# A decoder layer whose query projection is done in seven block products instead of eight

## The chip, the cores and the metric

The kernel runs on one core of one Trainium2 chip. The metric is the device time of one execution in microseconds (us), lower is better. A few words of the text: TensorE, VectorE, ScalarE, GpSimd and SyncE are the core's engines (PE, DVE, ACT, POOL and SP in the rows; PEld is the load of weights into TensorE). Each has a queue of its own that it works off in order, and they wait for one another by semaphores. SyncE issues all the transfers here. PSUM is TensorE's output memory, in 8 banks of 128 x 512 float32; SBUF is the working memory.

## The reference

One pre-norm decoder layer over 2 batches of 512 tokens, 1024 wide: self-attention, a quantised product with a context, and a mixture of 64 low-rank experts. What matters for the change is the attention:

```python
q = (hidden_states @ Wq.T).reshape(b, s, H, D)          # 32 heads of 128
kc, vc = hidden_states @ Wk_down.T, hidden_states @ Wv_down.T
k, v = k_cmp @ Wk_up.T, v_cmp @ Wv_up.T                 # from the latents: 8 heads of 128
scores = q @ k.T / sqrt(D)                              # causal, 4 query heads share a key head
out = softmax(scores) @ v
x = x + out @ Wo.T
```

After it come `x + fake_quant(layernorm(x)) @ fake_quant(ctx)` and `x + ffn(layernorm(x))`, which the change leaves as they are.

## The kernel before

**Numbers.** Every float32 operand of the attention is held as two float16 parts, a rounded one ("hi", made by ScalarE, L594) and the remainder ("lo", made by VectorE from the source and the hi part, L855). `split_product` (L1245) multiplies hi by hi, hi by lo and lo by hi, so each block of 128 rows takes three matmuls.

**Stages.** First the layer norm, the turning of its result into `h_t` and the down projection to the latents `lat` (TensorE until 69 us in the profile). Then eight groups, one a key head, the first and the last written out and the six in the middle in a loop; then the rest of the output projection, and the two later layers.

**A group** has 8 steps (`UNITS`), one for each of its four query heads and two batches. In step u TensorE does in this order (`group`, L1394):

- `scores(g, u)`: 12 matmuls into banks 0 to 2, which need the queries of unit u and the keys;
- `outputs(g, u - 2)`: probabilities times values for the unit of two steps ago, 15 matmuls into bank 5;
- two chunks of the output projection, `wo_chunk`: 6 matmuls of 512 columns each, over a pair of heads that is complete, mostly of the group before;
- `q_product(u + 2)`: the queries that are used two steps later, 24 matmuls of 512 columns;
- two more chunks.

Chunks, query products and the keys and values share four banks in rotation (`GEN_BANK`); a product waits until the one four uses back is read. In step 1 the group's values come in ahead of the chunks (two products `v_product`), in step 7 the keys of the next group (`k_product`). The order of the uses is written down by `step_uses`. In the first group there are no chunks before step 6, and in the last one no query products after step 5.

**Beside it.** VectorE in step u: `maxima(u)` (scores and mask to `prob`, row maxima, then `neg_max`, L1012), `p_split(u - 1)` (the remainder of the probabilities, 1280 columns), the add of the first chunk to `x_sb` (`wo_add`, L993), `inverses(u)` (L980), `o_split(u - 2)`, the add of the second chunk, a weight split of 1024 columns in most steps (`wq_sb` in even, `wo_sb` in odd ones), at times a context rounding or a smaller split, the query remainder, and two adds. ScalarE does the hi parts and the exponentials in between. GpSimd multiplies the exponentials by the inverses (L565), clips a context chunk (L546) in two steps and adds one to a column sum (L554) in two. The probabilities are then turned by two DMA transpositions a unit (`turn`, hi and lo), both on SyncE's queue, which also loads weights and context chunks between them.

**At the group's ends.** `scores(g, u + 1)` waits for `neg_max` of u (its banks), `outputs` for both transpositions and for `o_split` of the unit before (bank 5), and `outputs` of the first unit for the values.

## Time and profile before

| | us |
|---|---|
| median of 3 runs (1149.09 to 1150.87) | 1150.37 |
| the profiled execution | 1148.15 |
| its span, first to last instruction | 1146.4 |
| TensorE busy | 1111.4 (97%) |
| VectorE busy | 760.0 (66%) |
| ScalarE busy | 487.8 (43%) |
| GpSimd busy | 260.1 (23%) |
| granted TensorE clock, mean | 0.995 |

The busy times are sums over the whole span; an average says little of a stage. The chain of waits goes back from the last instruction, at each step to what released it; an engine's share of it is the time in which the end hung on that engine. TensorE's matmuls overlap, so a row of 12 matmuls that is 2.75 us long gives way to the next after 2.59 us: what a piece costs is read from one start to the next.

### The profile page before, as it was taken

The numbers are of one execution on the slowest core, as the hardware profiler recorded it, in microseconds if no ns is written. First come the engines' busy times: TensorE is split into PE (matmuls) and PEld (weight loads), VectorE is DVE, ScalarE is ACT, GpSimd is POOL, SyncE is SP. The second block draws the span as 40 slices with busy tenths as digits, with TensorE's granted clock in tenths as the row PEclk, the third lists the DMA queues.
The fourth block names the chain that finished last, engine by engine and source line by source line (L and its number), as shares of the span: only waits on it lengthen the run. The fifth ranks groups of instructions, "written<-read, shape, count | busy, mean of one in ns | idle before, by whom it ended". The sixth has DMA issues, their size and how long they took to land.

```text
span 1146.4 us, 18967 instructions
## 1 busy us (share of the span) xinstructions
PE 1111.4 (97%) x6541; PEld 599.0 (52%) x6548; DVE 760.0 (66%) x1670; ACT 487.8 (43%) x986; POOL 260.1 (23%) x323
## 2 busy tenths in 40 slices
PE   4999999999999999999999999999999998799997
PEld 4965555555555555555555555555555554345553
DVE  6746766656665666566666666666666687888853
ACT  4636644444444444434443444344434452343421
POOL 2003522322232223222322232223222321000000
PEclk9999999999999999999999999999999999999999
DMA  8014743444344434443444344434443457000001
GB/s 324 1 46 88 180 120 72 113 101 120 75 108 101 119 80 103 101 119 82 101 101 119 82 101 101 119 82 101 101 111 83 102 113 209 1 1 37 25 32 55
DMA packets 189996, 109.72 MB, mean 96 GB/s; under 512 B 170369, under 2 KB 170497, under 8 KB 189953
## 3 DMA queue, kind: packets, MB, share of 16 engines
q1 hardware_dynamic: 189952, 109.15, 37.4%
q8 instruction: 26, 0.43, 0.2%
q14 instruction: 18, 0.14, 0.0%
HBM read 58.80 MB, written 8.39 MB: 59 GB/s over the span
## 4 chain that ended last, share of the span: by engine, by line
PE 94%; DVE 3%; DMA 1%; ACT 1%; issue 0%; SPq 0%; POOL 0%; DVEq 0%; POOLq 0%; ACTq 0%
PE ps L1245 89%; PE ps L1453 3%; PE ps L1469 1%; PE ps L1520 1%; PE ps L1259 1%; DVE stats L863 1%; DMA o_t<-in_wdown 0%; DMA wq_in<-in_a_w 0%; DMA prob_t<-prob_s 0%; PE ps L1529 0%; DVE x_sb L1175 0%; POOL prob L565 0%; PE ps L1499 0%; ACT prob L645 0%; DVE prob L1006 0%
## 5 line engine op out<-in xcount | busy, mean ns | idle before, releaser
L1245 PE MATMUL ps<-wo_sb,o_t 128*128 128x512 f16 x1536 | 350.6, 379 | 3.6 <-DVE x_sb L993 3.6
L1245 PE MATMUL ps<-h_t,wq_sb 128*128 128x512 f16 x1536 | 341.8, 379 | 0.0
L565 POOL TENSOR_SCALAR prob<-prob,row_inv 128x128 f32<-128x128 f32 (+3 forms) x256 | 193.3, 774 | 633.2 <-DVE row_inv L980 633.2
L1245 PEld LDWEIGHTS ps<-h_t,wq_sb 128*128 128x128 f16 x1536 | 150.1, 98 | 179.6
L1245 PEld LDWEIGHTS ps<-wo_sb,o_t 128*128 128x128 f16 x1536 | 148.0, 98 | 172.6 <-DVE x_sb L993 4.1
L729 ACT ACTIVATE prob<-prob,neg_max 128x128 f32<-128x128 f32 (+3 forms) x256 | 140.6, 550 | 209.4 <-DVE neg_max L1012 209.2
L993 DVE SCALAR_TENSOR_TENSOR x_sb<-ps,x_sb 128x512 f32<-128x512 f32 x256 | 174.8, 687 | 57.7 <-PE ps L1245 57.5
L855 DVE SCALAR_TENSOR_TENSOR q_t<-ps,q_t 128x512 f16<-128x512 f32 x72 | 49.7, 691 | 199.7 <-ACT q_t L594 199.5
L594 ACT ACTIVATE q_t<-ps 128x512 f16<-128x512 f32 x72 | 43.0, 598 | 273.6 <-PE ps L1245 268.9
L1006 DVE CUSTOM_DVE_ANT_0 prob<-ps,mask 128x512 f32<-128x512 f32 (+3 forms) x256 | 112.8, 488 | 6.8 <-issue 1.5
L1245 PE MATMUL ps<-prob_t,v_sb 128*128 128x128 f16 (+2 forms) x960 | 115.3, 273 | 0.2 <-DMA prob_t<-prob_s 0.2
L1245 PE MATMUL ps<-k_t,q_t 128*128 128x512 f16 (+3 forms) x768 | 114.8, 299 | 0.0
L1245 PEld LDWEIGHTS ps<-prob_t,v_sb 128*128 128x128 f16 x960 | 83.1, 98 | 29.3 <-DMA prob_t<-prob_s 0.5
L855 DVE SCALAR_TENSOR_TENSOR prob_s<-prob,prob_s 128x1280 f16<-128x1280 f32 x64 | 95.0, 1485 | 0.0
L1245 PEld LDWEIGHTS ps<-k_t,q_t 128*128 128x128 f16 x768 | 67.0, 98 | 50.7
L594 ACT ACTIVATE prob_s<-prob 128x1280 f16<-128x1280 f32 x64 | 80.9, 1264 | 4.9 <-POOL prob L565 3.7
L855 DVE SCALAR_TENSOR_TENSOR o_t<-ps,o_t 128x512 f16<-128x512 f32 x64 | 44.3, 692 | 19.5 <-ACT o_t L594 19.5
L1245 PE MATMUL ps<-h_t,wo_sb 128*128 128x256 f16 x384 | 45.5, 282 | 3.1 <-DVE h_t L855 3.1
L729 ACT ACTIVATION_READ_ACCUMULATOR prob<-prob,neg_max 128x1 f32 x256 | 47.8, 187 | 0.0
L855 DVE SCALAR_TENSOR_TENSOR wo_sb<-wo_in,wo_sb 128x1024 f16<-128x1024 f32 x32 | 43.9, 1371 | 0.5 <-ACT wo_sb L594 0.5
L1245 PE MATMUL ps<-b_sb,q_t 128*128 128x512 f16 x192 | 42.8, 379 | 1.4 <-DVE q_t L855 1.4
L1245 PEld LDWEIGHTS ps<-h_t,wo_sb 128*128 128x128 f16 x384 | 38.6, 101 | 9.0 <-DVE h_t L855 3.5
(116 smaller groups left out, 886.4 us busy)
## 6 DMA issues: line engine op xcount, KB each, us to landing
wq_in<-in_wq SPq DMA_DIRECT2D x32, 512.0 KB, 4.2
wo_in<-in_wo SPq DMA_DIRECT2D x32, 512.0 KB, 3.8
side_in<-in_ctx SPq DMA_DIRECT2D x16, 512.0 KB, 3.6
x_sb<-in_x SPq DMA_DIRECT2D x8, 512.0 KB, 8.9
ctx_quantised<-side_out SPq DMA_DIRECT2D x16, 256.0 KB, 2.4
h_t<-ctx_quantised SPq DMA_DIRECT2D x2, 2048.0 KB, 9.9
out<-x_sb SPq DMA_DIRECT2D x8, 512.0 KB, 2.6
o_t<-in_wdown SPq DMA_DIRECT2D x4, 512.0 KB, 8.1
```

The costliest lines, as they stand in the source:

```text
L565: ins = nc.gpsimd.tensor_scalar(at, at, row_inv[:, u % 2, q:q + 1], S_P, ALU.mult, ALU.mult)
L594: nc.scalar.activation(dst, src, ACT.Copy, scale=scale).then_inc(signal, 1)
L729: ins = nc.scalar.activation(at, at, ACT.Exp, bias=neg_max[:, n % 2, q:q + 1], scale=SOFTMAX, accum_out=row_sum[:, n % 2, q:q + 1])
L855: nc.vector.scalar_tensor_tensor(dst, src, scale, hi, ALU.mult, ALU.subtract).then_inc(signal, 1)
L863: ins = nc.vector.bn_stats(stats[:, n, j, :], x_sb[:, t, j * HALF:(j + 1) * HALF])
L993: nc.vector.scalar_tensor_tensor(at, ps[:, bank, :], WO_OUT, at, ALU.mult, ALU.add).then_inc(gen_read, 1)
L1006: ins = nc.vector.tensor_tensor_reduce(prob[:, u % 2, at:at + width], ps[:, at // HALF, at % HALF:at % HALF + width], mask[:, SEQ - width: ...
L1245: ins = nc.tensor.matmul(out_, lhs(i), rhs(j), start=start and n == 0, stop=stop and n == 3 * len(pairs) - 1)
L1259: ins = nc.tensor.transpose(ps[:, 2 * (t % 2) + j, k * P:(k + 1) * P], hn[:, t % 2, at:at + P], ident[:, :])
L1453: ins = nc.tensor.matmul(ps[:, X_BANK[j], :], x_qt[:, t % 2, k * P:(k + 1) * P], ctx_q[:, b, k, j * HALF:(j + 1) * HALF], start=k == 0, st ...
L1469: ins = nc.tensor.matmul(ps[0:2 * ROUTER, SMALL_BANK, R_COL:R_COL + P], router_sb[:, k, :, :].rearrange("p a r -> p (a r)"), h3_t[:, t % 2 ...
L1520: ins = nc.tensor.transpose(ps[:, H_BANK[j], k * P:(k + 1) * P], h3[i % 2][:, at:at + P], ident[:, :])
```

## The change

**Seven products.** Take the weights of two query heads, split in half along the 1024 inputs, as a 2 x 2 matrix of blocks A11, A12, A21, A22 (128 x 512 each), and the normalised input, split in the same halves and by batch, as B11 to B22. The four results (two heads, two batches) are 8 block products. The new kernel takes 7, with sums of blocks on both sides (the Strassen-Winograd form), and adds the products up afterwards. A block product is 12 matmuls of 512 columns (4 blocks of 128 by three passes). Seven make a *cycle*, which gives 4 units; there are 15 cycles, each spread over four steps as 2, 2, 2 and 1 products. The first 4 units are done plainly, 24 matmuls each.

**Right-hand sums** T1 to T4 (of B11, B12, B21, B22, hi and lo parts) are made once, by GpSimd: 10 sums of 128 x 512 for each of 4 blocks of rows, one after another, each four results split in two by ScalarE and VectorE. **Left-hand sums** of the weights: GpSimd, four sums a cycle.

**Adding up.** ScalarE copies the first product out of PSUM; VectorE's `combine` adds a product to a running sum in SBUF (`q_tmp`), 7 a cycle, which also sets the query's bank free. From the sums ScalarE and VectorE make the queries' two parts (`q_part`), 4 a cycle.

**Banks and order.** The queries have banks 4 and 3, the chunks banks 6 and 7. In each step TensorE does the query products right after `outputs`, and then all four chunks; chunk i waits until chunk i - 2 is added. VectorE's adds come after its splits and combinations of the step, and the query parts after the adds.

**Keys and values** of all 8 key heads are computed ahead of the first group, seven of them written to DRAM (`kv_parts`), that of the first group last and kept. Keys are loaded again in step 7 of the group before, values in step 1 of the group. Weight parts of the second expert product go to DRAM as well and are loaded at the end. Weights of the queries are loaded and split in halves of 512 columns, seven splits a cycle of 512 in place of four a group of 1024.

The core of the diff; left out are ScalarE's side of the splits, which follows VectorE's order, the buffers' new places and the loads:

```diff
-GEN_BANK = (4, 3, 6, 7)
+WO_BANK = (6, 7)
...
+RIGHT = ("B11", "T2", "B21", "T3", "T1", "T4", "B22")
+SUMS = ((1, 0, 1), (2, 0, 0), (3, 1, 2), (4, 2, 0), (4, 1, 1), (5, 2, 2), (6, 1, 1))
+STEP_SUMS = ((0,), (1, 2), (3, 4, 5), (6,))
+UNIT_SUM = {0: 1, 3: 3, 2: 5, 1: 6}
+STEP_UNITS = ((), (0,), (3, 2), (1,))
+STEP_PRODUCTS = ((0, 1), (2, 3), (4, 5), (6,))
+BLOCK_SLOT = (0, 1, 2, 3, 0, 1, 2)
+A11, A12, A21, A22 = range(4)
+Q_BANK = (4, 3)
+CYCLES = 2 * KV_HEADS - 1
+KV_USES = (("k", 0), ("v", 0), ("k", 1), ("v", 1))
+PLAIN_Q = 4
...
         @block.gpsimd
...
+                chain = ((0, hi(b12), ALU.subtract, hi(b11)), (0, None, ALU.add, lo(b12)), (0, None, ALU.subtract, lo(b11)),
+                         (1, hi(b22), ALU.subtract, q_tmp[:, 0, :]), (1, None, ALU.add, lo(b22)),
+                         (2, hi(b21), ALU.subtract, q_tmp[:, 1, :]), (2, None, ALU.add, lo(b21)),
+                         (3, hi(b22), ALU.subtract, hi(b12)), (3, None, ALU.add, lo(b22)), (3, None, ALU.subtract, lo(b12)))
+                for i, (place, left_, op, right) in enumerate(chain):
+                    done = T_OPS * n + i
...
+            def wq_sum_1(m):
+                pool.wait_ge(wq_lo, 7 * m + 2)
+                pool.wait_ge(wq_loaded[A21], 16 * m + 32)
+                pool.wait_ge(wq_loaded[A22], 16 * m + 32)
+                nc.gpsimd.tensor_tensor(q_tmp[:, SUM_TMP, :], wq_in[:, A21, :], wq_in[:, A22, :], ALU.add)\
+                    .then_inc(wq_summed, 1)
+                pool.wait_ge(wq_summed, 4 * m + 1)
+                pool.wait_ge(wq_loaded[A11], 16 * m + 32)
+                nc.gpsimd.tensor_tensor(wq_in[:, A21, :], wq_in[:, A11, :], wq_in[:, A21, :], ALU.subtract)\
+                    .then_inc(wq_summed, 1)
+            def wq_sum_2(m):
+                pool.wait_ge(wq_lo, 7 * m + 5)
+                pool.wait_ge(wq_summed, 4 * m + 2)
+                nc.gpsimd.tensor_tensor(wq_in[:, A11, :], q_tmp[:, SUM_TMP, :], wq_in[:, A11, :], ALU.subtract)\
+                    .then_inc(wq_summed, 1)
...
+                    if u % PAIR_UNITS == 0 and not (last and u >= PAIR_UNITS):
+                        wq_sum_4(m)
+                    if u % PAIR_UNITS == 2 and not last:
+                        wq_sum_1(m + 1)
+                    if u % PAIR_UNITS == 3 and not last:
+                        wq_sum_2(m + 1)
...
         @block.vector
...
+            def combine(g, u, n):
+                m = 2 * g + u // PAIR_UNITS
+                product, src, dst = SUMS[n]
+                dve.wait_ge(prod_done, 7 * m + product + 1)
+                if n == 0:
+                    dve.wait_ge(p1_copied, m + 1)
+                    dve.wait_ge(q_lo, 4 * m + 4)
+                    if kind_of(g) == "first" and u < PAIR_UNITS:
+                        dve.wait_ge(t_lo, 16)
+                else:
+                    dve.wait_ge(combined, 7 * m + n)
+                if n == 3:
+                    dve.wait_ge(q_lo, 4 * m + 5)
+                nc.vector.scalar_tensor_tensor(q_tmp[:, dst, :], ps[:, Q_BANK[product % 2], :], Q_OUT, q_tmp[:, src, :],
+                                               ALU.mult, ALU.add).then_inc(combined, 1)
...
+                    queries = not (last and u >= PAIR_UNITS)
+                    s = u % PAIR_UNITS
                     maxima(g, u)
                     if not (first and u == 0):
                         p_split(g, u - 1)
                     inverses(g, u)
                     if not (first and u < LAG):
                         o_split(g, u - LAG)
+                    if queries and s == 0:
+                        block(2, g, u)
+                        block(3, g, u)
+                    if queries and s == 1:
+                        block(4, g, u)
+                        block(5, g, u)
+                    if queries and s == 2:
+                        block(6, g, u)
+                    if s == 3 and not last:
+                        block(0, g, u)
                     if u == 1 and not first:
                         wo_split(g, -1)
                     if u in (3, 5, 7):
...
                         a_split(u - 4)
                     if u == 2:
                         ctx_round(g, 0)
                     if u == 4:
                         b_split(g)
                     if u == 7:
                         ctx_round(g, 1)
+                    if queries:
+                        for n in STEP_SUMS[s]:
+                            combine(g, u, n)
+                    for i in range(WO_STEP):
+                        step_add(g, u, i)
+                    if queries:
+                        for unit in STEP_UNITS[s]:
+                            q_part(g, u, unit)
+                    if s == 3 and not last:
+                        block(1, g, u)
...
         @block.tensor
...
+            def query_product(g, u, i):
+                m = 2 * g + u // PAIR_UNITS
+                pe.wait_ge(wq_lo, 7 * m + 5 + i)
+                begins = kind_of(g) == "first" and u < PAIR_UNITS
+                if i < 2 and begins:
+                    pe.wait_ge(q_lo, PLAIN_Q)
+                    pe.wait_ge(gen_read, 2 * DOWN + 4 * KV_HEADS)
+                    pe.wait_ge(t_lo, 16)
+                elif i < 2:
+                    pe.wait_ge(combined, 7 * m - i)
+                elif i == 2:
+                    pe.wait_ge(p1_copied, m + 1)
                 else:
-                    bank = bank_free(g, what)
-                if c == 0:
-                    pe.wait_ge(wo_lo, DOWN + 4 * (g - before) + 2 * pair + 2)
-                if c in (0, WO_CHUNKS // 2):
-                    pe.wait_ge(o_lo, UNITS * (g - before) + 4 * pair + 3 + 2 * c // WO_CHUNKS)
+                    pe.wait_ge(combined, 7 * m + (0, 0, 0, 1, 2, 3, 5)[i])
+                split_product(ps[:, Q_BANK[i % 2], :],
+                              [(lambda a, k=k: wq_sb[:, BLOCK_SLOT[i], a, k * P:(k + 1) * P],
+                                lambda c, k=k: h_b[:, H_BLOCK[RIGHT[i]], c, k, :])
+                               for k in range(KT // 2)]).then_inc(prod_done, 1)
...
+            def wo_chunk(g, u, i):
+                pair, before, chunks = wo_span(kind_of(g) == "first", u)
+                if len(chunks) == 0:
+                    return
+                if kind_of(g) == "first" and u == UNITS - 2 and i < 2:
+                    pe.wait_ge(q_lo, PLAIN_Q)
+                else:
+                    pe.wait_ge(wo_read, wo_number(g, u, i) - 2)
+                wo_inputs(g - before, pair, chunks[i])
+                wo_product(WO_BANK[i % 2], pair, chunks[i])
...
-                    for what in step_uses(kind_of(g), u):
-                        if what[0] == "wo":
-                            wo_chunk(g, what)
-                        elif what[0] == "q":
-                            if u % 2 == 0:
-                                pe.wait_ge(wq_lo, 4 * g + (u + LEAD) // 2 + 1)
-                            bank = bank_free(g, what)
-                            q_product(u + LEAD, bank, 0)
-                            q_product(u + LEAD, bank, 1).then_inc(gen_done, 1)
-                        elif what[0] == "v":
-                            v_product(what[1], bank_free(g, what)).then_inc(gen_done, 1)
-                        else:
-                            if what[1] == 0:
-                                pe.wait_ge(up_lo, g + 2)
-                            k_product(what[1], bank_free(g, what)).then_inc(gen_done, 1)
+                    if not (kind_of(g) == "last" and u >= PAIR_UNITS):
+                        for i in STEP_PRODUCTS[u % PAIR_UNITS]:
+                            query_product(g, u, i)
+                    for i in range(WO_STEP):
+                        wo_chunk(g, u, i)
```

## Rows read from the trace of the kernel before

**Rows 1.** The page: busy times, and the chain that ended last.

```profile
PE 1111.4 (97%) x6541; PEld 599.0 (52%) x6548; DVE 760.0 (66%) x1670; ACT 487.8 (43%) x986; POOL 260.1 (23%) x323
PE 94%; DVE 3%; DMA 1%; ACT 1%; issue 0%; SPq 0%; POOL 0%; DVEq 0%; POOLq 0%; ACTq 0%
```

**Rows 2.** Groups by line: count, busy, mean ns, idle before and its releaser.

```profile
L1245 PE MATMUL ps<-h_t,wq_sb 128*128 128x512 f16 x1536 | 341.8, 379 | 0.0
L1245 PE MATMUL ps<-wo_sb,o_t 128*128 128x512 f16 x1536 | 350.6, 379 | 3.6 <-DVE x_sb L993 3.6
L993 DVE SCALAR_TENSOR_TENSOR x_sb<-ps,x_sb 128x512 f32<-128x512 f32 x256 | 174.8, 687 | 57.7 <-PE ps L1245 57.5
```

**Rows 3.** Windows: a middle group; busy of PE, PEld, DVE, ACT, POOL, clock, DMA.

```profile
505.14:619.43 114.29, 114.29 (x661) 59.55 (x660) 73.72 (x152) 49.03 (x104) 30.30 (x36) 1.00 0.41 101
```

**Rows 4.** Timeline, TensorE, step 3 of that group: start, length.

```profile
548.70 1.79 PE L1245 MATMUL ps<-k_t,q_t 128*128 128x512 f16 x12
550.33 1.80 PE L1245 MATMUL ps<-prob_t,v_sb 128*128 128x128 f16 x15
551.97 2.75 PE L1245 MATMUL ps<-wo_sb,o_t 128*128 128x512 f16 x12
554.56 5.34 PE L1245 MATMUL ps<-h_t,wq_sb 128*128 128x512 f16 x24
559.74 2.75 PE L1245 MATMUL ps<-wo_sb,o_t 128*128 128x512 f16 x12
```

**Rows 5.** Timeline, TensorE: first scores, end of the first group, last group.

```profile
84.64 1.79 PE L1245 MATMUL ps<-k_t,q_t 128*128 128x512 f16 x12
162.27 1.79 PE L1245 MATMUL ps<-k_t,q_t 128*128 128x512 f16 x12
848.01 1.79 PE L1245 MATMUL ps<-k_t,q_t 128*128 128x512 f16 x12
940.90 1.79 PE L1245 MATMUL ps<-k_t,q_t 128*128 128x512 f16 x12
```

**Rows 6.** Timeline, TensorE and VectorE: the end of the down projection.

```profile
69.01 10.52 PE L1245 MATMUL ps<-h_t,wq_sb 128*128 128x512 f16 x48
70.79 1.73 DVE L905 SCALAR_TENSOR_TENSOR lat<-ps,lat 64x256 f16<-64x256 f32 x4 [0.89 <-ACT lat L637]
```

**Rows 7.** Transfers: the page's issues, and SyncE's queue in step 3.

```profile
wq_in<-in_wq SPq DMA_DIRECT2D x32, 512.0 KB, 4.2
556.05 0.33 SPq L408 DMA_DIRECT2D wq_in<-in_wq  x1
```

**Rows 8.** By line, GpSimd's two-input sum: duration min/median/max.

```profile
L554 POOL TENSOR_TENSOR ctx_sum<-ctx_sum,side_out x16: 2115/2119/2122, 116.7 to 955.3; 128x1024 f16<-128x1024 f16 x16
```

**Rows 9.** Timeline, TensorE and VectorE, step 1 of the middle group.

```profile
518.77 1.79 PE L1245 MATMUL ps<-k_t,q_t 128*128 128x512 f16 x12
524.16 0.18 DVE L980 RECIPROCAL row_inv<-row_sum 128x4 f32<-128x4 f32 x1 [0.97 <-ACT prob L729]
524.64 0.69 DVE L855 SCALAR_TENSOR_TENSOR o_t<-ps,o_t 128x512 f16<-128x512 f32 x1 [0.30 <-ACT o_t L594]
525.25 1.28 DVE L855 SCALAR_TENSOR_TENSOR v_sb<-ps,v_sb 128x512 f16<-128x512 f32 x2
```

**Rows 10.** Weight splits beside GpSimd: timeline of both, and the mean.

```profile
528.12 1.85 DVE L855 SCALAR_TENSOR_TENSOR wo_sb<-wo_in,wo_sb 128x1024 f16<-128x1024 f32 x1
527.85 1.04 POOL L546 TENSOR_SCALAR side_in<-side_in 128x1024 f32<-128x1024 f32 x1 [1.25 <-ACT side_in L682]
105.41 1.41 DVE L855 SCALAR_TENSOR_TENSOR wq_sb<-wq_in,wq_sb 128x1024 f16<-128x1024 f32 x1 [0.25 <-ACT wq_sb L594]
L855 DVE SCALAR_TENSOR_TENSOR wo_sb<-wo_in,wo_sb 128x1024 f16<-128x1024 f32 x32 | 43.9, 1371 | 0.5 <-ACT wo_sb L594 0.5
```

**Rows 11.** Timeline, VectorE and TensorE: from remainder to values, unit 0.

```profile
95.11 1.49 DVE L855 SCALAR_TENSOR_TENSOR prob_s<-prob,prob_s 128x1280 f16<-128x1280 f32 x1
100.26 1.81 PE L1245 MATMUL ps<-prob_t,v_sb 128*128 128x128 f16 x15 [0.20 <-DMA prob_t<-prob_s]
```

762 lines of the change are left out of this document (474 added, 288 removed).

## The prediction

> **What bounds the kernel now.** I read the busy line and the chain of waits first: TensorE is busy 97% of the span and owns 94% of the chain that ended last [rows 1]. Then the groups by line: the 1536 query matmuls and the 1536 output matmuls never wait, but for one wait of 3.6 us on a VectorE add [rows 2]. A middle group of 114.29 us is TensorE through and through at full clock, with VectorE 73.72 and GpSimd 30.30 us beside it [rows 3]. The timeline shows why. A step is scores 1.63, probability times values 1.64, two chunks 2.59, a query product 5.18, two chunks 2.59, together 13.63 us [rows 4]. VectorE evicts chunks while the query product runs, and four banks rotate. So a matmul taken away is time won only while VectorE stays ahead of TensorE, and the cover that lets it is the query product between the chunks.
>
> **Matmuls removed.** 64 query units of 24 matmuls become 4 plain ones and 15 cycles of 7 products of 12: 1536 against 96 + 1260 = 1356. 180 fewer at 5.18/24 = 0.216 us is 38.8 us off TensorE.
>
> **Keys and values moved ahead.** 84.64 - 69.01 less two query units (10.36) is 5.27 us a head [rows 5, 6]. This is moved, not removed. The stretch from 69.01 to the first scores becomes 8 x 5.27 + 4 x 5.18 = 62.9. The first head's product for batch 1 comes after 2.6 us of work, but its latent is ready at 70.79 + 1.73 = 72.52 [rows 6]; two query units hid that until now. So 0.9 more, 63.8 against 15.6: **+48.2**. VectorE there has, a head, 4 evictions, one weight split and two T splits, 7 x 0.60 = 4.2 of 5.27 us (0.69 long, 0.60 from one to the next), ScalarE less. Both stay hidden. The loads of keys and values back (512 KB) are issued some 7.5 us into a step, as the weight load of this size at 548.70 + 7.35; at 4.2 us they land at about 12 [rows 4, 7], the scores that need keys start at 14, the values are needed at 15. I cost them at nothing; without that cover each is a us or two a group.
>
> **GpSimd's sums ahead.** 40 sums of 128x512 for the T blocks. The trace has no such float32 sum; the nearest row is a float16 one of 1024 columns, 2.12 us [rows 8]. By elements that is 1.06 us, and a whole 2.12 is the upper end; a sum cannot gain time. The chain runs ten sums for four T splits, which are spread over two heads (10.5 us). At 1.06 it keeps pace and its last split comes before the plain queries end. At 2.12 each chain needs 21 us, the last splits come some 13 us late, and the evictions of queries behind them hold the first scores: 0 to +13. I take 0, by size.
> The Trainium skill (GPSIMD Engine Reference, Elementwise, side-by-side cycle accounting) puts a float32 sum of 2048 elements at 4497 ns. By it 512 elements are an estimated 1.1 us and the term is 0 too; no row here shows it.
>
> **A long step after the change** (three of four). Work for TensorE: 1.63 + 1.64 + 5.18 for two products, then four chunks one after another, 5.18. Only banks 6 and 7 are left for chunks, so the third may not start before the first is added, at +8.45 + 2.59 = +11.04. VectorE's order is maxima, remainder of probabilities, inverses, remainder of outputs, weight splits, combinations, adds, query remainders. By the step at 518.77 the inverse starts at +5.39, and VectorE is free at +6.48 [rows 9]. In step 1: two block splits 1.2, an output-weight split behind ScalarE's to about +9.1, two combinations 1.2 to +10.3, add to +11.0. It just fits; steps 0 and 2 come out at 10.6 to 10.8, late start counted. The step stays 13.63.
>
> **A short step** (the fourth). One product, so TensorE has 11.04 us of work and wants the third chunk at 5.86 + 2.59 = +8.45. VectorE starts late, as the last add ends at +0.8 and two query remainders of step 2 follow: first maximum at +2.0 instead of +1.0. Everything shifts by 1.0: free at +7.45, block split to 8.05, output-weight split (ScalarE hands over at 8.35) to 9.5, combination to 10.1, add to 10.9. Wait 2.45; step 7 has a rounding of 0.6 as well, 3.05. Adds and query remainders cost what their rows do (0.69, 0.60 apart) [rows 2].
> Splits read two SBUF tiles, and with GpSimd at its normalisation they stretch: 1.85 us beside GpSimd's 1.04 us clip, 1.41 beside a normalisation [rows 10]. The new splits start 0.35 us earlier after the inverse than that one did, into GpSimd's third piece. Between 0 and 0.5 a step; I take 0.25, thus 2.7 and 3.3, and 0.2 in each of steps 1 and 5, which had no slack.
> The Trainium skill (SBUF - State Buffer, Who interferes with whom) says that a VectorE instruction with two SBUF inputs and a GpSimd one that reads SBUF exclude each other for a whole instruction. By that rule the stretch is up to a whole GpSimd piece at each meeting, which speaks for the upper end. The stretched rows agree in kind.
>
> **Edits costed at nothing.** ScalarE's copy of the first product and its 14 block splits of some 0.6 for 4 of 1.05: ScalarE is busy 43% [rows 1] and a step ahead of the product that needs them; without that cover a product waits 0.6. GpSimd's four weight sums a cycle, at 1.06 each, stand behind a normalisation that ends near +10; the one that is urgent, for the second product of the next cycle, is split by ScalarE and VectorE at the end of step 3, two microseconds and more ahead of that product at +5.9 of the next. It makes VectorE start its maxima at +2.0 there too, which step 0 bears (first add 10.6). SyncE's queue gets two more loads a cycle (256 KB halves), one store of the second-layer expert weights and one reload a group, all behind the second transposition, so transpositions are late only if a wait ahead of them is; all their waits name work a step old. The reload of the second-layer weights at the end, 2 x 1 MB behind 2 MB of context, has 40 us until its first matmul.
>
> **Middle group:** 6 x 13.63 + 2 x 11.04 = 103.86, waits 6.4: 110.3 against 114.29, six times: **-24**.
>
> **First group.** Without waits 2 x 6.81 + 3 x 8.45 + 5.86 + 13.63 + 11.04 = 69.5. VectorE has up to 9 us a step here. From remainder of probabilities to values takes 100.26 - 96.60 = 3.7 us [rows 11], and the whole chain from scores to values 15.6 us [rows 5, 11], which two steps with a short one among them (14.3) don't cover. Unit 2: its remainder of probabilities ends at 30.2 after the first scores, as VectorE comes to its maxima of step 3 at 26.8 only; values from 33.9, TensorE is there at 30.7. Going on like this I get waits of 1, 3 and 2 us before the values of units 0, 2 and 3, 1 in step 6, 3.3 in step 7, 0.7 of splits: 80.5 against 77.63: **+3**.
>
> **Last group.** Steps 0 to 3: 40.9 + 11.04 + 2.1. Steps 4 to 7 have no product at all: 8.44 of work each, the third chunk wanted at +5.86, while VectorE after +6.48 (+7.06 in step 4, behind a query remainder) has splits of 1.13 each (1, 2, 1, 2 of them), in step 4 a 0.6 split and in step 7 a 0.6 rounding, so that the first add ends at 9.8, 9.8, 8.7 and 10.4: waits 4.0, 3.9, 2.8 and 4.5, and 0.5 for stretched splits. Sum 103.5 against 940.90 + 8.44 - 848.01 = 101.3 and the 3.6 us wait behind it, which goes, as the first-layer expert weights are now loaded two steps earlier [rows 2, 5]: **-1.5**. What is late next after it is the outputs of unit 6, with 2 us of slack.
>
> **Sum:** +48.2 + 3 - 24 - 1.5 = +25.5; the same by the other road, -38.8 + 0.9 + 11.0 + 38.4 + 17.8 - 3.6 = +25.7. The profiled execution took 1148.15 us (span 1146.4 and 1.75 around it), so 1174; it lies 2.2 below the median, which becomes **1176 us**.
>
> **Rivals.**
> 1. *The exclusion decides.* GpSimd pieces hold splits and query remainders 0.5 us or more at every meeting, and all eight steps wait. For it: the 1.85 us row. Against: the output-weight splits average 1.37 over all 32 [rows 10]. Waits 7.5 to 9 a middle group, 3 more at both ends: 1188.
> 2. *The sums ahead are slow*, 2.12 us each: +13, 1189. Against it is only the scaling by size.
> 3. *Not slower: the adds are in time.* Place: the third chunk of the twelve short steps of the middle groups. The waits elsewhere are 0.9 + 11.0 + 17.8 - 3.6 = 26.1, so it decides at (38.8 - 26.1)/12 = 1.1 us a short step. If VectorE started these steps without lag, the first add would end at 6.48 + 0.6 + 1.13 + 0.6 + 0.69 = 9.5, a wait of 1.05, 1.65 in step 7, and the first and last groups would lose 5 and 3 less: sum -5, 1146. For it: VectorE is idle a third of a group and never held TensorE but once. Against: the query remainders stand behind adds that wait for TensorE.
> 4. *The saving doesn't come*, as the matmul count doesn't fall: the loops say 1356, so under 1 in 100.
>
> **Chances.** Forecast 0.55, with its own range 1164 to 1185; rival 1 0.21, rival 2 0.09, rival 3 0.15. In the range of 8 in 10 I go to 1150, over the middle of rival 3, and to 1191. Within 0.2% (2.3 us, about what a measurement here can tell from none) lies the edge of rival 3: 0.03. Faster 0.11, slower 0.86.
>
> **What would show it.** 1356 query matmuls. First scores at 132.8 us. Middle groups near 110.3, with TensorE waiting 2 to 3.5 us on a VectorE add ahead of the third chunk in steps 3 and 7 and next to nothing in the others; steps 4 to 7 of the last group 11 to 13 us each. GpSimd's sum near 1.1 us. Wrong would be: middle groups under 106 (rival 3), waits in the long steps (rival 1), ScalarE waiting for GpSimd ahead of the first scores (rival 2), or waits on the loads of keys.

## The result, and the profile after

The changed kernel takes **1189.26 us** (median, 1186.54 to 1189.60) against 1150.30 in the same comparison: a ratio of 1.0335, 95% interval 1.0317 to 1.0353, so 39 us slower. The forecast was 1176 with a range of 1150 to 1191: the direction is right, the time lies inside the range, and it is 13 us above the forecast, which is what most of the experiments are about. Unless a row or a span is named, times are medians, each with its own runs of the kernel before (1149.1 to 1150.3).

The page of the changed kernel, as [rows 1, 2]; its profiled span is 1187.5 us.

```profile
PE 1091.8 (92%) x6361; PEld 581.6 (49%) x6368; DVE 888.9 (75%) x1868; ACT 537.3 (45%) x1094; POOL 416.2 (35%) x423
PE 67%; DVE 13%; ACT 10%; issue 7%; DMA 1%; DVEq 0%; POOL 0%; SPq 0%; ACTq 0%; POOLq 0%
L1533 PE MATMUL ps<-wo_sb,o_t 128*128 128x512 f16 x1536 | 357.7, 388 | 53.8 <-DVE x_sb L1279 53.3
L1533 PE MATMUL ps<-h_b,wq_sb 128*128 128x512 f16 x1524 | 341.4, 380 | 0.0
L1279 DVE SCALAR_TENSOR_TENSOR x_sb<-ps,x_sb 128x512 f32<-128x512 f32 x256 | 173.9, 688 | 113.9 <-PE ps L1533 113.2
```

TensorE had 97% of the span and waited 3.6 us ahead of output matmuls; now it has 92% and waits 53.8 us there, nearly all for `x_sb`, VectorE's adds. The group of query matmuls never waits. It holds 1524, since 192 matmuls of the first-layer expert weights now read a part of `h_b`, and 24 query matmuls read B12 as `wo_in`: 1524 - 192 + 24 = 1356, the number of the prediction.

Where the parts end, by TensorE's timeline (start, length), as [rows 5]: first scores, end of the first group, last group, first matmul behind the output projection.

```profile
135.92 1.80 PE L1533 MATMUL ps<-k_t,q_t 128*128 128x512 f16 x12
220.93 1.79 PE L1533 MATMUL ps<-k_t,q_t 128*128 128x512 f16 x12
882.68 1.79 PE L1533 MATMUL ps<-k_t,q_t 128*128 128x512 f16 x12
1028.79 0.61 PE L1821 MATMUL ps<-ident_b,prob_t 128*128 128x128 bf16 x8
```

Before the change the matmul of the last row was this one; the table has the stretches in us.

```profile
987.50 0.61 PE L1493 MATMUL ps<-ident_b,prob_t 128*128 128x128 bf16 x8
```

| Stretch | Before | After | Difference | Forecast |
|---|---|---|---|---|
| to the first scores | 84.64 | 135.92 | +51.3 | +48.2 |
| first group | 77.63 | 85.01 | +7.4 | +3 |
| six middle groups | 685.74 | 661.75 | -24.0 | -24 |
| last group and the outputs behind it | 139.49 | 146.11 | +6.6 | -1.5 |
| the rest | 158.9 | 158.7 | -0.2 | 0 |

A short step, as [rows 4]: first TensorE, then VectorE from the first maximum on.

```profile
593.00 1.79 PE L1533 MATMUL ps<-k_t,q_t 128*128 128x512 f16 x12
594.63 1.80 PE L1533 MATMUL ps<-prob_t,v_sb 128*128 128x128 f16 x15
596.27 2.75 PE L1533 MATMUL ps<-h_b,wq_sb 128*128 128x512 f16 x12
598.86 2.75 PE L1533 MATMUL ps<-wo_sb,o_t 128*128 128x512 f16 x12
603.85 2.76 PE L1533 MATMUL ps<-wo_sb,o_t 128*128 128x512 f16 x12 [2.24 <-DVE x_sb L1279]
```

```profile
595.01 0.69 DVE L1297 CUSTOM_DVE_ANT_0 prob<-ps,mask 128x512 f32<-128x512 f32 x1
...
599.30 0.18 DVE L1268 RECIPROCAL row_inv<-row_sum 128x4 f32<-128x4 f32 x1 [0.96 <-ACT prob L968]
599.78 0.69 DVE L1091 SCALAR_TENSOR_TENSOR o_t<-ps,o_t 128x512 f16<-128x512 f32 x1 [0.30 <-ACT o_t L741]
600.39 0.68 DVE L1091 SCALAR_TENSOR_TENSOR wq_sb<-wq_in,wq_sb 128x512 f16<-128x512 f32 x1
601.25 1.34 DVE L1091 SCALAR_TENSOR_TENSOR wo_sb<-wo_in,wo_sb 128x1024 f16<-128x1024 f32 x1 [0.18 <-ACT wo_sb L741]
602.51 0.68 DVE L1255 SCALAR_TENSOR_TENSOR q_tmp<-ps,q_tmp 128x512 f32<-128x512 f32 x1
603.12 1.27 DVE L1279 SCALAR_TENSOR_TENSOR x_sb<-ps,x_sb 128x512 f32<-128x512 f32 x2
```

The first chunk is done at 601.45, but VectorE comes to its add at 603.12, and the third chunk starts when that is done. The maxima start at +2.01 and the add at +10.12; the timetable of the prediction had +2.0 and +10.1. A bracket counts idle time only: from one chunk's start to the next this wait is 4.99 us for 2.59, so it costs 2.40 us and not 2.24, and the other waits are 0.16 us dearer than their brackets in the same way.

**What the sum missed.** Three rows more of TensorE's timeline. The 12 matmuls of a chunk take 2.76 us, 36 take 7.93.

```profile
328.27 4.45 PE L1533 MATMUL ps<-wo_sb,o_t 128*128 128x512 f16 x12 [2.83 <-DVE x_sb L1279]
439.65 2.76 PE L1533 MATMUL ps<-wo_sb,o_t 128*128 128x512 f16 x12 [2.83 <-DVE x_sb L1279]
989.05 10.73 PE L1533 MATMUL ps<-wo_sb,o_t 128*128 128x512 f16 x36 [4.96 <-DVE x_sb L1279]
```

Behind some of the waits the matmuls ran at 1.2 GHz (the granted clock is 0.50 of full speed from 960.9 to 964.0, and 1.00 from 439.7 to 442.0), for some 3 to 6 us. There are seven such places: 1.7 us too long in all in the first group, 3.1 in the middle groups, 7.8 in the last. Without them the first group is +5.7, a middle group 109.8 and the last part -1.2. The span grew by 41.1 us where the sum had 25.5. Of these 15.6 us the clock is 12.6, the front 3.1, the first group's own waits 2.7, the last part 0.3, and the middle groups give 3.1 back. (The terms as written, +48.2 + 3 - 24 - 1.5, add up to 25.7 and not to 25.5; 0.2 us is rounding.)

### The profile page after: what moved, and what is told of

It reads as the page before. It is cut to its first block, busy times and chain, and to the rows that moved or that the text cites. A ratio compares the mean times of both kernels' runs of the same rounds, so it can differ in the third digit from the quotient of the medians.

```text
span 1187.5 us, 19870 instructions
## 1 busy us (share of the span) xinstructions
PE 1091.8 (92%) x6361; PEld 581.6 (49%) x6368; DVE 888.9 (75%) x1868; ACT 537.3 (45%) x1094; POOL 416.2 (35%) x423
## 4 chain that ended last, share of the span: by engine, by line
PE 67%; DVE 13%; ACT 10%; issue 7%; DMA 1%; DVEq 0%; POOL 0%; SPq 0%; ACTq 0%; POOLq 0%
PE ps L1533 62%; ACT prob L968 4%; DVE prob L1297 3%; PE ps L1781 3%; ACT wo_sb L741 2%; DVE x_sb L1279 2%; DVE q_tmp L1255 2%; ACT wq_sb L741 1%; DVE h_b L1091 1%; DVE wo_sb L1091 1%; ACT o_t L741 1%; DVE stats L1099 1%; PE ps L1797 1%; PE ps L1849 1%; DMA o_t<-in_wdown 1%
## 5 line engine op out<-in xcount | busy, mean ns | idle before, releaser
L1533 PE MATMUL ps<-wo_sb,o_t 128*128 128x512 f16 x1536 | 357.7, 388 | 53.8 <-DVE x_sb L1279 53.3
L705 POOL TENSOR_SCALAR prob<-prob,row_inv 128x128 f32<-128x128 f32 (+3 forms) x256 | 218.8, 872 | 495.5 <-DVE row_inv L1268 495.5
L1533 PE MATMUL ps<-h_b,wq_sb 128*128 128x512 f16 x1524 | 341.4, 380 | 0.0
L1533 PEld LDWEIGHTS ps<-h_b,wq_sb 128*128 128x128 f16 x1524 | 146.1, 98 | 165.1 <-issue 1.0
L741 ACT ACTIVATE q_t<-q_tmp 128x512 f16<-128x512 f32 x60 | 37.8, 630 | 91.0 <-DVE q_tmp L1255 91.0
L1255 DVE SCALAR_TENSOR_TENSOR q_tmp<-ps,q_tmp 128x512 f32<-128x512 f32 x105 | 72.0, 686 | 6.0 <-PE ps L1533 1.3
L1091 DVE SCALAR_TENSOR_TENSOR wq_sb<-wq_in,wq_sb 128x512 f16<-128x512 f32 x94 | 67.6, 733 | 0.5 <-ACT wq_sb L741 0.3
L735 POOL TENSOR_TENSOR rstd<-var_eps,minus_half 128x1 f32<-128x1 f32 x16 | 8.8, 548 | 154.4 <-DVE var_eps L1102 154.4
L741 ACT ACTIVATE wq_sb<-wq_in 128x512 f16<-128x512 f32 x94 | 56.6, 619 | 6.3 <-POOL wq_in L664 6.3
L1268 DVE RECIPROCAL row_inv<-row_sum 128x4 f32<-128x4 f32 x64 | 11.4, 178 | 62.9 <-ACT prob L968 62.9
```

The lines of the kernel that those rows point to most:

```text
L705: ins = nc.gpsimd.tensor_scalar(at, at, row_inv[:, u % 2, q:q + 1], S_P, ALU.mult, ALU.mult)
L741: nc.scalar.activation(dst, src, ACT.Copy, scale=scale).then_inc(signal, 1)
L1091: nc.vector.scalar_tensor_tensor(dst, src, scale, hi, ALU.mult, ALU.subtract).then_inc(signal, 1)
L1255: nc.vector.scalar_tensor_tensor(q_tmp[:, dst, :], ps[:, Q_BANK[product % 2], :], Q_OUT, q_tmp[:, src, :], ALU.mult, ALU.add).then_inc(com ...
L1533: ins = nc.tensor.matmul(out_, lhs(i), rhs(j), start=start and n == 0, stop=stop and n == 3 * len(pairs) - 1)
```

## Experiments

The prediction's theory is that VectorE comes late to the first add where too little of TensorE's work covers it. The expectations call it A where they name theories; its rivals differ from kernel to kernel and are named there.

**1. Split order.** Two chunks ahead of the query products and two behind, as before the change; VectorE's adds follow: one ahead of the inverses, one behind the outputs' remainder. The seven products stay.

```diff
+                    for i in range(2):
+                        wo_chunk(g, u, i)
                     if not (kind_of(g) == "last" and u >= PAIR_UNITS):
...
-                    for i in range(WO_STEP):
+                    for i in range(2, WO_STEP):
                         wo_chunk(g, u, i)
```

> Edit: the changed kernel with two of a step's four chunks put back ahead of the query products, and VectorE's first add ahead of the inverses, the second right after the remainder of the outputs. Nothing of the work changes: same products, same two chunk banks, keys and values in DRAM. Theory A (the saving was lost because the third chunk waits for VectorE's first add, which stands behind splits and combinations): the waits in steps 3 and 7 go, middle groups fall from 110.3 to 104 us, the last group and what is behind it from 146 to about 122, the first from 85 to 80; 1189 - 38 - 24 - 5 = 1122 us. Theory B (VectorE, with 75% busy and locked against GpSimd, is the bound itself, in whatever order): the waits move to other places, middle groups stay at 108 or more, 1165 to 1190. Theory C (keys and values ahead and their reload cost what is lost): 1180 to 1190.

Measured 1132.97 us (ratio 0.9861, 0.9837 to 0.9884): 56 us less than the changed kernel and 1.4% less than the kernel before. No middle group waits for an add any more. The place of the chunks and of their adds turned the gain into the loss. It missed A's 1122 by 11, and TensorE's timeline has a new wait at the start of each group:

```profile
427.46 1.80 PE L1535 MATMUL ps<-k_t,q_t 128*128 128x512 f16 x12 [1.06 <-DMA k_t<-kv_parts]
```

There are seven of them, 8.1 us in all: the keys' load stood behind both transpositions of step 7 in SyncE's queue (issued at 423.02) and takes 4.2 to 4.4 us. In the changed kernel the wait for the add had hidden it.

**2. Adds first, VectorE's order alone.** The chunks stay behind the products; in the short steps and in steps 4 to 7 of the last group VectorE adds chunks 0 and 1 right behind the outputs' remainder, ahead of splits and combination.

```diff
                         o_split(g, u - LAG)
+                    tight = s == 3 or not queries
+                    if tight:
+                        step_add(g, u, 0)
+                        step_add(g, u, 1)
```

> Edit: only VectorE's order. In steps 3 and 7, and in steps 4 to 7 of the last group, it does the adds of the first two chunks right after the remainder of the outputs, ahead of splits, combinations and rounding; TensorE's order is that of the changed kernel, chunks last. Theory A: the third chunk of a short step is wanted at +8.45 and the first add now ends near +8.2, so middle groups come to about 104 us; steps 4 to 7 of the last group still wait some 1.3 us each (chunk wanted at +5.86, add ends at +7.2), without the slow clock behind it: 1189 - 38 - 18 - 5 = 1128 us. Theory B: no gain, as VectorE's work is the same, 1170 to 1190. If TensorE's order itself costs (its products ahead of the chunks, whatever VectorE does): above 1150.

Measured 1160.67 us (ratio 1.0096, 1.0079 to 1.0112): 29 us of the 39 back, but 32 above the 1128 that A gave it. TensorE's timeline, a short step and the long one behind it (the scores of both, and the long step's chunks):

```profile
368.49 1.79 PE L1537 MATMUL ps<-k_t,q_t 128*128 128x512 f16 x12
379.52 1.79 PE L1537 MATMUL ps<-k_t,q_t 128*128 128x512 f16 x12
387.97 2.75 PE L1537 MATMUL ps<-wo_sb,o_t 128*128 128x512 f16 x12
392.66 2.76 PE L1537 MATMUL ps<-wo_sb,o_t 128*128 128x512 f16 x12 [1.94 <-DVE x_sb L1279]
```

The short step takes 11.03 us, without any wait. But VectorE now comes to the long step's maxima at +4.33, not +2.0:

```profile
378.34 1.22 DVE L1091 SCALAR_TENSOR_TENSOR wo_sb<-wo_in,wo_sb 128x1024 f16<-128x1024 f32 x1
379.48 0.68 DVE L1255 SCALAR_TENSOR_TENSOR q_tmp<-ps,q_tmp 128x512 f32<-128x512 f32 x1
380.08 1.27 DVE L1279 SCALAR_TENSOR_TENSOR x_sb<-ps,x_sb 128x512 f32<-128x512 f32 x2
381.27 2.05 DVE L1091 SCALAR_TENSOR_TENSOR q_t<-q_tmp,q_t 128x512 f16<-128x512 f32 x1
383.25 0.68 DVE L1091 SCALAR_TENSOR_TENSOR wq_sb<-wq_in,wq_sb 128x512 f16<-128x512 f32 x1
383.85 0.68 DVE L1297 CUSTOM_DVE_ANT_0 prob<-ps,mask 128x512 f32<-128x512 f32 x1
```

The work that the adds overtook runs into the next step, a query remainder meets a GpSimd sum (2.05 us for 0.68), and the long step waits 1.94 us. Most of the wait of the short step was passed on, not removed. The same holds behind step 7: the next group starts with a wait of 0.67 to 1.39 us for its keys, seven times and 7.3 us in all, and its step 0 waits 0.2 to 1.0 us more for an add. A's cause was right and its account of one step at a time was not.

**3. Filler.** The changed kernel with throwaway matmuls ahead of the third chunk, in the waits of steps 3 and 7 and of the last group (8 to 22 a time, 235 in all). They read the second chunk's inputs and write to a query bank that is idle then; nobody reads their results.

```diff
                     for i in range(WO_STEP):
+                        if i == 2:
+                            filler(g, u)
                         wo_chunk(g, u, i)
```

> Edit: the changed kernel with extra matmuls whose results nobody reads (11 in step 3, 13 in step 7, 17, 18, 13 and 22 in steps 4 to 7 of the last group, 512 columns each, into the idle query bank), put ahead of the third chunk, where TensorE waits for VectorE's add. They fill the wait and take nothing away from VectorE. The output is unchanged. Theory A with a price of the clock: behind waits of 2.8 us and more the chunks ran slow in two of the middle groups (12 matmuls 4.4 and 4.2 us instead of 2.76) and in each step 4 to 7 of the last group (4.3 to 4.5, and 10.7 instead of 7.9 for 36), 3 and 8 us together; with TensorE kept busy these go and the waits stay as they are: 1189 - 10 = 1178 to 1180 us, granted clock of the last group back from 0.94 to 1.00. If the clock isn't set by the waits: 1189 to 1194, and the slow chunks stay.

Measured 1177.56 us (ratio 1.0239, 1.0222 to 1.0256): 235 matmuls more and 11.7 us less. The last group by windows (columns as in [rows 3]), in the changed kernel and in this one:

```profile
883.00:987.00 104.00, 88.78 (x480) 44.37 (x477) 74.83 (x153) 46.67 (x100) 32.27 (x36) 0.95 0.48 112
```

```profile
883.00:1010.00 127.00, 126.58 (x682) 62.80 (x680) 94.92 (x186) 50.84 (x104) 36.38 (x39) 1.00 0.55 144
```

The granted clock is 0.95 there and 1.00 here, and no chunk of a middle or the last group is slow any more. So the slow matmuls cost about what their rows say (10.9 us in these groups), and they go when TensorE doesn't stand still. The middle groups still take 109.7 us: filling a wait doesn't shorten it.

**4. The kernel before with its chunks late.** All four chunks behind the query product and VectorE's adds all behind its splits, four banks as they were, no seven products.

```diff
-    order += wo[:WO_STEP // 2]
     if not (last and u + LEAD >= UNITS):
         order.append(("q", u + LEAD))
-    return order + wo[WO_STEP // 2:]
+    return order + wo
```

> Edit: the kernel before, with a step's query product ahead of all four chunks and VectorE's adds all after the splits, the order of the changed kernel, but with its own eight query products, 13.63 us steps and four banks in rotation. Theory A (order costs only where the step is short and the banks two): the fourth chunk waits for the query remainder, done near +9.8 and wanted at +12.3, so no waits in the groups; 1150, and up to 1154 for the wait behind the last group, which grows from 3.6 to some 6 us. If the order alone costs: 2 us or more a step, 1190 and above.

Measured 1153.68 us (ratio 1.0032, 1.0021 to 1.0042). 114 us of the middle groups, as [rows 3]:

```profile
240.00:354.00 114.00, 114.00 (x661) 59.44 (x659) 76.02 (x153) 49.01 (x105) 29.74 (x36) 1.00 0.41 101
```

TensorE is busy throughout, so the order alone costs a middle group nothing. It takes the short step, in which 2.59 us of product and two banks are all that covers VectorE. How much of this is the short product and how much the two banks was not tested apart. What this kernel loses lies behind the last group, where no query product stands between the chunks: one wait there is 7.28 us where it was 3.62, and the matmuls behind it are slow.

```profile
957.48 8.19 PE L1244 MATMUL ps<-wo_sb,o_t 128*128 128x512 f16 x24 [7.28 <-DVE x_sb L992]
```

**5 and 6. A doubled split, in short and in long steps.** One weight split is made twice: block 0 (steps 3 and 7, 14 times) or block 3 (steps 0 and 4, 15 times).

```diff
+                if i == 0:        # or 3
+                    dve.wait_ge(wq_hi, number)
+                    nc.vector.scalar_tensor_tensor(...).then_inc(twice, 1)
+                    dve.wait_ge(twice, m + 1)
+                block_split(place, BLOCK_SLOT[i], number)
```

> The changed kernel, with VectorE doing one weight split twice in each short step (block 0, in steps 3 and 7; 14 times in all), everything else as it was. Theory A, VectorE's chain ahead of the first add sets the third chunk of the short steps: the second copy is one more split of 0.60 us behind a semaphore, some 0.65; in the changed kernel's step at 593.00 VectorE stood idle for 0.18 us behind this split, until ScalarE handed over the output weights, and that comes off: 0.47 to 0.65 a short step, 14 x = 6.6 to 9 us, so 1196 to 1198, with waits of 2.7 to 2.9 us in step 3 and 3.3 to 3.5 in step 7; up to 10 us more if TensorE's clock falls behind more of these longer waits. Rival B, VectorE's time costs the same wherever it stands, as it is busy 75% of the span: this kernel and its twin with the long steps both become 9 us slower. Rival C, the waits are made by ScalarE or by a transfer: no change, 1189.

> The twin of the kernel with the doubled split in the short steps: here the doubled split is block 3, in steps 0 and 4, which are long steps (15 times). Theory A: by the timetable of the prediction the first add ends in these steps at 10.6 to 10.8 us and is wanted at 11.04, so a doubled split of 0.65 costs 0.2 to 0.4 a time at most, and nothing where a step had more slack: 0 to 5 us in all, 1189 to 1194. Rival B (VectorE's time costs the same everywhere): +9, 1198, as its twin. Rival C: 1189 in both.

Measured 1223.43 us (ratio 1.0646) and 1215.45 us (1.0570): 34 and 26 us more than the changed kernel. All three theories missed, the long steps above all. VectorE and TensorE in the long-step kernel, just behind the turn of the loop over groups:

```profile
453.47 0.69 DVE L1304 CUSTOM_DVE_ANT_0 prob<-ps,mask 128x512 f32<-128x512 f32 x1 [3.40 <-issue]
```

```profile
462.31 2.76 PE L1540 MATMUL ps<-wo_sb,o_t 128*128 128x512 f16 x12 [3.12 <-DVE x_sb L1286]
```

VectorE stood 3.40 us in "issue", with scores at hand. Such a gap of 2.6 to 3.7 us is there at all five turns in both kernels; the changed kernel has none at its turns, and its largest elsewhere in the loop, in step 5, is 0.46. So these two measured something else than they were made for.

**7 and 8. The same dose without one more instruction.** The split writes its 512 columns and 512 more to a spare place, as one instruction of 1024 columns.

```diff
+                if i == 0:        # or 3
+                    place, hi = (at.unsqueeze(1).to_broadcast([P, 2, HALF]) for at in (place, hi))
+                    lo = wq_sb[:, slot:5:4 - slot, 1, :]
```

> The doubled split of the short steps again, but without one more instruction: VectorE's split of block 0 writes its 512 columns and 512 more to a spare place, as one instruction of 1024 columns (some 1.28 us for 0.69), in steps 3 and 7. With the second instruction and its semaphore the run took 1223.4 us, and VectorE stood 2.6 to 3.7 us in 'issue' at each turn of its loop, where the changed kernel has 0.2 to 0.5 in three of six groups; the page counts 46 packets in the second instruction queue there, 21 in the changed kernel. Theory A: the longer loop no longer fitted where VectorE's instructions are held, and the gap is the fetch; the dose itself costs only what it adds to the waits of steps 3 and 7 (there 2.23 to 2.83 and 2.83 to 3.85 us). So here: 21 packets, no gap, no wait of 1.5 us in the step behind the turn, and 14 x 0.5 to 1.0 = 7 to 12 us more than the changed kernel's 1189, 1196 to 1201; and up to 20 more, 1221, if TensorE runs at half its clock behind each of these waits, as it did behind 10 of them there (+1.6 us each). Rival B: the gap comes from VectorE's longer work: it stays, 1223. Rival C: no cost, 1189.

> The twin: the split of block 3, in the long steps 0 and 4, as one instruction of 1024 columns. With a second instruction it took 1215.5 us, with 'issue' gaps of 2.6 to 3.5 us at each loop turn and waits of 2.3 to 3.2 us in step 0 behind them, while step 4 waited 0.23 us at most. Theory A: without the gap both steps have slack for 0.6 us: 0 to 0.3 us each, 0 to 4 us in all, 1188 to 1193, 21 packets. Rival B (the gap comes from VectorE's longer work): 1213 to 1216. Rival C (VectorE's time costs the same everywhere): as much above 1189 as its twin in the short steps.

Measured 1197.13 us (1.0422, 1.0404 to 1.0439) and 1193.83 us (1.0386, 1.0369 to 1.0403): 8 us for the short steps, as A has it, 4.6 for the long ones, just over its 4; the gaps are gone. In the short steps the waits grew from 2.23 to 2.38 and from 2.83 to 3.29, 14 times 0.3 on average and some slow matmuls more; in the long steps one wait of 0.17 us a group came, in step 4 (2.92 us from chunk to chunk for 2.59), step 0 took the dose for nothing, and the rest is more slow matmuls. Both are well under the 0.6 that VectorE had more to do: part of it fell into VectorE's waits for ScalarE. Per dose the short steps cost twice the long ones; the two intervals only just stand apart, so the rows carry this more than the medians.

**9. Waits only.** The changed kernel with eight semaphore waits more a loop, all passed already and each with its counting instruction, and no data work.

```diff
+                if i == 0:
+                    for _ in range(4):
+                        dve.wait_ge(wq_hi, number)
+                        dve.sem_inc(dve_passed)
```

> The changed kernel with no work added, but eight more semaphore waits that have passed already, each with its counting instruction, ahead of VectorE's split of block 0 in steps 3 and 7 (four each). It asks what the 'issue' gaps of 2.6 to 3.7 us at VectorE's loop turn hang on, which were there when a second split with its semaphore wait stood in the loop (46 packets in the second instruction queue) and not when the same 512 columns more were in one longer instruction (21 packets, 0.2 to 0.5 us in three of six groups). Theory A, the number of instructions in VectorE's loop: the gaps come back with 40 packets and more, step 0 waits 1.5 to 3 us on an add as it did there, 6 x 1.5 to 3 and some half-clock chunks: 1198 to 1215. Rival B, it hangs on the second data instruction or its semaphore: 21 packets, no gap; eight waits of some 0.05 us cost at most 0.5 us a group: 1189 to 1193.

Measured 1205.17 us (1.0486, 1.0469 to 1.0504). VectorE at one turn, and the page's row of the second instruction queue (packets, MB, share); the changed kernel and kernels 7 and 8 have 21 packets and 0.17 MB.

```profile
451.39 0.69 DVE L1302 CUSTOM_DVE_ANT_0 prob<-ps,mask 128x512 f32<-128x512 f32 x1 [1.55 <-issue]
...
q14 instruction: 46, 0.38, 0.1%
```

Kernels 5 and 6 have 46 packets as well. Five turns and 25 packets more, five a turn. That instructions are fetched again at each turn once the loop is this long is read from this count and the gaps; no row shows which engine's instructions the packets carried. A is right in kind; the gaps are 1.55 to 1.81 us, smaller than before, and step 0 waited 0.37 to 0.62 only. The rest of the 16 us is in steps 3 and 7 (2.39 and 3.40 us, as the waits themselves take VectorE's time there) and in slow matmuls behind the latter. The Trainium skill (Runtime: NRT & Kernel Launch, Instruction fetch mechanics) says that crossing a block of instructions is mostly hidden, but that a taken branch to a target outside the two pages held makes the engine wait for that page. The rows agree in kind: the gaps stand at the loop's turns, 1.6 to 3.7 us each.

**10. Short sums.** The changed kernel with GpSimd's 40 sums for the T blocks cut to 64 of 512 columns. The other columns stay zero, so this kernel leaves out most of that work and computes something else.

```diff
-                    return block[:, 0, n, :]
+                    return block[:, 0, n, 0:64]
...
-                    at = q_tmp[:, place, :]
+                    at = q_tmp[:, place, 0:64]
```

> The changed kernel with GpSimd's 40 sums for the T blocks cut from 512 to 64 columns each (the other 448 columns of each T block are left zero, so this leaves work out), all else as it was. It asks why the first scores came at 135.92 us and not at 132.8. Theory A: VectorE's splits that read two SBUF tiles were stretched by GpSimd's 512-column sums beside them (1.02 and 1.28 us mean for 0.69); with sums of some 0.3 us they come back to 0.7 to 0.8, the waits of 0.77, 0.37, 0.68 and 0.68 us ahead of the keys' and values' products go, and the first scores come at 133.0 to 133.5: total 2.5 to 3 us less, 1186 to 1187. Rival B: VectorE has too many operations there whatever GpSimd does (or the evictions of PSUM set it): the splits of two SBUF tiles stay over 1 us or the waits stay, first scores at 135.5 to 136, 1189.

Measured 1186.82 us (1.0326, 1.0309 to 1.0343). VectorE's splits of two SBUF tiles, by line: the changed kernel, then this one.

```profile
L1091 DVE SCALAR_TENSOR_TENSOR h_b<-q_tmp,h_b 128x512 f16<-128x512 f32 x16 | 16.0, 1021 | 9.8 <-ACT h_b L741 9.8
L1091 DVE SCALAR_TENSOR_TENSOR prob_t<-prob_t 128x512 f16<-128x512 f32 x8 | 10.3, 1284 | 0.0
```

```profile
L1094 DVE SCALAR_TENSOR_TENSOR h_b<-q_tmp,h_b 128x512 f16<-128x512 f32 x16 | 10.3, 682 | 0.0
L1094 DVE SCALAR_TENSOR_TENSOR prob_t<-prob_t 128x512 f16<-128x512 f32 x8 | 5.7, 715 | 2.5 <-ACT prob_t L744 2.4
...
133.79 1.80 PE L1536 MATMUL ps<-k_t,q_t 128*128 128x512 f16 x12
```

Three of the four waits in the front are gone (0.37, 0.68, 0.68 us) and the first scores come at 133.79 in place of 135.92. A holds for three waits of four: GpSimd's sums stretched VectorE's splits. The wait of 0.77 us stays, and the first scores come 0.3 us behind A's range. The total can't be told from the changed kernel's by its interval, so the rows decide.

**11. Keys earlier.** The split order with the keys' load between the two transpositions of step 7.

```diff
                 sp.dma_start_transpose(prob_t[:, buf, 0, :, :], prob_s[:, 0, :]).then_inc(p_turned[buf], 16)
+                if keys is not None:
+                    load_k(keys)
```

> The split order (two chunks ahead of the products and two behind, 1132.97 us) with one thing more: SyncE issues the load of the next group's keys between the two transpositions of step 7 and not behind both. In the split-order kernel TensorE waited 0.7 to 1.9 us for keys at the start of 7 groups, 8.1 us in all; the load was issued 7.7 us after the step's scores began and took 4.2 to 4.4 us to land. Theory A: issued some 5 us earlier it lands in time, all seven waits go and nothing takes their place: 1125. Rival B: the load holds up the second transposition, and with it the values of the next step, by the 0.4 us of its issue or its share of the DMA engines: waits on prob_t in their place, 1130 to 1133. Rival C: VectorE is late at these starts anyway, as it comes to the maxima last, so the waits pass to the third chunk: 1129 to 1133.

Measured **1122.83 us** (1121.47 to 1124.02; ratio 0.9763, 0.9747 to 0.9779), the fastest of all: 26 us under the kernel before. SyncE's queue and a middle group by windows, as [rows 3]:

```profile
415.42 0.36 SPq L507 DMA_DIRECT2D k_t<-kv_parts  x1
```

```profile
320.54:424.38 103.84, 103.84 (x577) 53.35 (x576) 86.81 (x172) 51.61 (x111) 42.77 (x45) 1.00 0.50 121
```

The group takes 103.84 us without a wait, where the prediction counted 103.86 of work, with VectorE at 84%.

**12. Values behind the products.** On top of that, in steps 0 to 5 of the first group TensorE computes the values after the query products.

```diff
-                    if not (first and u < LAG):
+                    late = first and u < UNITS - 2
+                    if not late:
                         outputs(g, u - LAG)
...
+                    if late and u >= LAG:
+                        outputs(g, u - LAG)
```

> Split order, keys loaded between the transpositions (1122.83 us), and one thing more: in steps 0 to 5 of the first group TensorE computes the values behind the query products, not ahead of them. There it waited 1.89, 2.97 and 2.32 us on the transposed probabilities and 0.67 on the maxima, and ran at half clock behind two of these waits (3.23 and 2.67 us for 15 matmuls that take 1.80). Theory A: a product of 5.2 us covers each of these waits; 7 us of waits and 2 us of slow matmuls go, less what comes back as VectorE gets the outputs later: 1114 to 1118. Rival B: VectorE's remainder of the outputs, and with it splits and combinations, come 5 us later, so that the waits pass to the third chunk or the next product: 1120 to 1124. Rival C: slower, as the late outputs hold the maxima of the following step: over 1125.

Measured 1125.47 us (0.9792, 0.9776 to 0.9808), 2.6 above kernel 11. The rows show B's mechanism, though the time lies just past B's range and in C's: the waits went over to the query products, whose banks VectorE empties late.

```profile
162.67 4.44 PE L1535 MATMUL ps<-h_b,wq_sb 128*128 128x512 f16 x12 [2.47 <-DVE q_tmp L1255]
173.51 7.03 PE L1535 MATMUL ps<-h_b,wq_sb 128*128 128x512 f16 x24 [3.14 <-DVE q_tmp L1255]
```

## Why the prediction was right, and where it was off

- *Matmuls removed* and *middle group*: right. -24.0 for -24, but partly by luck. From start to start the waits of the short steps cost 2.41 and 3.00 us for 2.7 and 3.3, and steps 1 and 5 lost 0.18 and 0.26 for 0.2 each: 0.5 us a group less than forecast, 3.1 in all. The slow matmuls, some 3 us as well and not in the prediction, made up for it.
- *Cause of the waits*: shown. VectorE reached its first maximum and the first add within 0.1 us of the timetable; taking the chunks back ahead of the product removed every wait (kernel 1, with the keys' load as the only new wait there), the order alone with four banks and a product of 5.18 us costs nothing (kernel 4), a dose of VectorE work costs in the short steps (kernel 7).
- *A long step*: right that it just fits. An extra 0.6 us (kernel 8) cost 0.3 in one of two.
- *Last group*: the waits were right (3.93, 4.11, 2.97, 5.12 from start to start for 4.0, 3.9, 2.8, 4.5 and 0.5 for stretched splits). The step that failed is that a wait costs only its own length: 7.8 us of matmuls at 1.2 GHz stood behind these. Filling the waits takes 11.7 us off the whole (kernel 3).
- *Keys and values moved ahead*: 3.1 too low. "Both stay hidden" failed: VectorE's 4.2 us of 5.27 a head were counted at 0.60 to 0.69 a split, and three kinds of them ran 1.0 to 1.6 beside GpSimd's sums (kernel 10). The exclusion of two SBUF inputs, which the prediction weighed for the steps, struck in the front, where it was not applied. Of the 3.1, 2.1 are shown; the first wait of 0.77 stays without the sums too.
- *GpSimd's sums*: 1.15 us alone and up to 1.69 beside VectorE, for the 1.06 taken. ScalarE did wait for them ahead of the first scores, seven times and 15.9 us in all, which the prediction had named as a sign of rival 2; but no wait of TensorE ended with them, so rival 2's +13 didn't come.
- *First group*: +5.7 without the clock for +3. The mechanism is right: from start to start the waits cost 2.0, 3.1 and 2.3 before values for 1, 3 and 2, 2.3 in step 6 for 1, 3.3 in step 7 for 3.3, and 0.8 on the maxima where 0.7 stood for splits. Unit 0 and step 6 were sized too low. For unit 0 the prediction took 3.7 us from the remainder of the probabilities to the values; here the values start at 153.19, 4.96 us after this row ends. What made it longer stays open.

```profile
146.74 1.49 DVE L1091 SCALAR_TENSOR_TENSOR prob_s<-prob,prob_s 128x1280 f16<-128x1280 f32 x1
153.19 1.81 PE L1533 MATMUL ps<-prob_t,v_sb 128*128 128x128 f16 x15 [1.85 <-DMA prob_t<-prob_s]
```

- *Loads of keys costed at nothing*: right here, yet only because a wait of 2.83 us stood ahead of it. "Without that cover each is a us or two a group" is what kernel 1 measured, 0.7 to 1.9.
- *Rivals*: rival 1's waits in all eight steps aren't in the rows; steps 0, 2, 4 and 6 of the middle groups have none. Rival 3, adds in time, is what kernels 1 and 11 made come true by another order, at 1133 and 1123 for its 1146.

## What to carry to other kernels

When matmuls are removed, the other engines have less time to hide behind. Count this cover and not only the work: what must VectorE finish before TensorE wants the next bank, in the shortest step? Put independent matmuls between a producer and its reuse, and check a reordering over two steps at least, as work that is overtaken lands in the next. A wait of some microseconds on TensorE may cost half as much again in slow matmuls behind it; and once a wait is gone, look for the load that it hid.

## What the hardware showed unasked

- **A few instructions more in VectorE's loop made it stand idle at each turn.** One split and its wait in each of two steps, or eight passed waits, brought 25 packets more on the instruction queue and gaps of 1.55 to 3.7 us, 16 to 34 us in all with what followed. The data work (kernels 7 and 8) brought neither. An experiment that adds an instruction must look at the issue gaps before its time is believed.
- **The clock behind waits is not regular.** Behind waits of 2.83 us the chunk took 2.76 us at 439.65 and 4.45 at 328.27, in the same place of the group; behind 3.40 us it was slow in all six middle groups (kernel 9), and once each already behind 2.38 (kernel 7) and 2.28 (kernel 6), while waits of 3.29 us three times were not followed by it (kernel 7). What else it hangs on stays open.
